# The end of a typed graph layer on one core: three stages become one stage whose engines work at different node blocks

## What is computed

```
h = relu(layernorm(x))
# per node: attention over incoming edges, softmax per edge type (6 relations, 4 heads); acc = sums over edges
t     = sum over present relations of acc / max(number present, 1)
trans = t @ Wa[type of node] + ba[type of node]            # 3 node types
out   = trans * alpha + h * (1 - alpha)                    # alpha = sigmoid(skip)[type of node]
norm  = layernorm(out) * ln_g[type] + ln_b[type]
x     = x + where(node has a message, norm, h)
h     = relu(layernorm(x))                                 # the next layer gathers rows of this h
```

## Time and profile before

| | us |
|---|---|
| median of 3 runs | 10156.97 (10148.26 to 10159.42) |
| profiled execution, its own time | 10223.11 |
| span of that execution | 10221.3 |

### The profile page before, as it was taken

One profiled execution on the slowest core, in us unless ns is written; L12 is line 12 of the kernel. 1 busy time (PEld: TensorE's weight loads), 2 busy tenths in 40 slices (PEclk: granted clock), 3 DMA queues, 4 the chain that ended last, 5 costly groups with the idle time before them and its releaser, 6 DMA issues. The chain is left out here.

```text
span 10221.3 us, 116388 instructions
## 1 busy us (share of the span) xinstructions
PE 6248.8 (61%) x25078; PEld 4724.2 (46%) x25079; DVE 5154.4 (50%) x8812; ACT 2241.4 (22%) x5049; POOL 4139.8 (41%) x4373
## 2 busy tenths in 40 slices
PE   4966676665434544788888888445555544555554
PEld 2545555554233333455555555344444433444443
DVE  3147777774323323555555555534444454444445
ACT  1211222211300000233333333322222222222221
POOL 0034554440076666333333333054444424444442
PEclk9977777777666666899999999766666666666666
DMA  2246666653032233333333333133333323333332
GB/s 91 97 148 180 189 192 175 188 170 84 12 98 86 86 92 86 99 102 102 102 104 107 102 102 103 41 111 100 99 96 100 101 54 100 101 98 103 102 102 72
DMA packets 439678, 1093.31 MB, mean 107 GB/s; under 512 B 102452, under 2 KB 177296, under 8 KB 439410
## 3 DMA queue, kind: packets, MB, share of 16 engines
q0 software_dynamic: 249344, 763.23, 26.9%
q1 hardware_dynamic: 190180, 328.60, 9.7%
HBM read 1009.55 MB, written 81.94 MB: 107 GB/s over the span
## 5 line engine op out<-in xcount | busy, mean ns | idle before, releaser
L781 POOL DMA_INDIRECT st_rows<-g_table,st_stage_idx x1632 | 1560.0, 956 | 1691.5 <-DVE st_msg L2339 1217.0
L2504 PE MATMUL st_psM<-st_msg,st_hot 128*128 128x273 f32 x3264 | 966.8, 458 | 423.1 <-DVE st_msg L2339 347.6
L882 POOL DMA_INDIRECT st_rows<-kv_table,st_stage_idx x832 | 827.5, 995 | 893.1 <-PE st_psM L1226 614.5
L2490 PE MATMUL st_psE<-st_side_alpha,st_hotrow 128*128 128x16 f32 x3264 | 694.9, 360 | 622.1 <-issue 605.1
L1831 PE MATMUL st_psC<-st_w,st_rT 128*128 128x256 f32 x3264 | 900.0, 423 | 225.5 <-ACT st_rT L1792 193.7
L2490 PEld LDWEIGHTS st_psE<-st_side_alpha,st_hotrow 128*128 128x128 f32 x3264 | 718.9, 328 | 674.4 <-issue 656.9
L2504 PEld LDWEIGHTS st_psM<-st_msg,st_hot 128*128 128x128 f32 x3264 | 714.7, 225 | 632.8 <-issue 238.2
L781 POOL DMA_INDIRECT st_rows<-h_table,st_stage_idx x816 | 832.5, 1020 | 429.1 <-issue 238.3
L712 POOL DMA_INDIRECT st_rows<-p_table,st_stage_idx x816 | 847.6, 1039 | 303.0 <-issue 221.2
L1831 PEld LDWEIGHTS st_psC<-st_w,st_rT 128*128 128x128 f32 x3264 | 634.3, 204 | 624.1 <-ACT st_rT L1792 403.0
L1727 DVE TENSOR_TENSOR st_pre<-st_psP,st_rows 128x512 f32<-128x512 f32 x816 | 526.9, 685 | 646.8 <-PE st_psP L1825 439.3
(11 more groups left out here) (407 smaller groups left out, 10111.2 us busy)
## 6 DMA issues: line engine op xcount, KB each, us to landing
st_dst_row<-in_dst_row SPq DMA_DIRECT2D x310, 512.0 KB
kv_table<-st_rows_out SPq DMA_DIRECT2D x25, 1560.0 KB, 5.6
st_ea<-in_ea SPq DMA_DIRECT2D x103, 256.0 KB
st_rows<-g_table,st_stage_idx POOLq DMA_INDIRECT x1632
st_pens<-pen_table SPq DMA_DIRECT2D x208, 72.0 KB
st_rows<-kv_table,st_stage_idx POOLq DMA_INDIRECT x832
st_rows<-h_table,st_stage_idx POOLq DMA_INDIRECT x816
st_rows<-p_table,st_stage_idx POOLq DMA_INDIRECT x816
```

Source lines behind the costliest of these rows:

```text
L781: pool.indirect_dma_start(out=rows[:, slot, j, :], out_offset=None, in_=table, in_offset=bass.IndirectOffsetOnAxis(ap=stage_idx[:, g, u * ...
L882: pool.indirect_dma_start(out=rows[:, slot, j, :], out_offset=None, in_=kv_table, in_offset=bass.IndirectOffsetOnAxis(ap=stage_idx[:, g, u ...
L2490: last = nc.tensor.matmul(expanded[:, j, u, :], onehots[:, j, :], alphas.rearrange("p n h -> p (n h)"), start=(fresh and j == 0), stop=Tru ...
L2504: last = nc.tensor.matmul(out[:, 0:MSG_W], onehots[:, j, :], msg[:, n, j, :], start=(j == 0), stop=(j == SLOTS - 1))
```

## The change

`typed_combine`, `finish_typed`, the `norm_stats` behind it and `store_normed` become one stage. Its loads go out in another order: the open values first, then half of the ends, `NODE`, `X` and the four arrays on SP's queue; the other half of the ends and all weights on ACT's queue. Each kind has its own semaphore. The sum over six relations becomes three additions. The scatter into `NODE` stays. Behind it every engine runs through 34 turns, unrolled; in turn k it works at block k minus a lag that differs by operation (PE 0, 1, 4; ACT 0, 1, 3, 4, 7, 8; DVE 2, 3, 5, 6, 7; POOL 3, 5), with two buffers each of `tm`, `tT`, `psT`, `psY` and `psG`. The choice between norm and `h` is made by multiplying with `has_msg` or `no_msg`; POOL does three elementwise operations a block. The product by `Wa` takes factors that already hold `alpha`, and the bias rows are scaled by it once. Type rows are used in place instead of copied. The store of the new `h` is the last step of a block. In the excerpt the indentation is shortened.

```diff
-  def typed_combine():
...
-    sp.dma_start(NODE[:, :, 0:SUM_W], acc_table[0:NPAD, :].rearrange("(b p) d -> p b d", p=P)).then_inc(S["node_in"], 16)
...
-    sp.dma_start(values[:, :, :, :].rearrange("s n r d -> s (n r d)"),
-          open_table.rearrange("s n d -> s (n d)")).then_inc(S["values"], 16)
-    sp.dma_start(X[:, :, :], a["x"].rearrange("(b p) d -> p b d", p=P)).then_inc(S["values"], 16)
-    sp.dma_start(src_idx[:, 0:NT], a["src"]).then_inc(S["values"], 16)
-    sp.dma_start(weight[:, 0:NT], a["weight"]).then_inc(S["values"], 16)
-    sp.dma_start(dst_rel[:, :], dst_rel_table).then_inc(S["values"], 16)
-    sp.dma_start(first[:, :], first_table).then_inc(S["values"], 16)
-    sp.wait_ge(S["values"], 16 * 6)
...
-      v.tensor_reduce(comb[:, side, D:SUM_W], values[:, side, :, D:SUM_W].rearrange("s r d -> s d r"), AX.X, ALU.add)
-      last = v.tensor_reduce(comb[:, side, 0:D], scaled[:, :, :].rearrange("s r d -> s d r"), AX.X, ALU.add)
...
-    with dve.Fori(0, NB) as b:
-      link.turn()
-      dve.wait_ge(S["h"], START + b + 1)
-      link(v.tensor_scalar(mix[:, :], h[:, block_of(b), :].squeeze(1), beta[:, ds(b, 1)], None, ALU.mult))
-      dve.wait_ge(S["trans"], START + b + 1)
-      v.scalar_tensor_tensor(NODE[:, block_of(b), 0:D].squeeze(1), psY[:, 0:D], alpha[:, ds(b, 1)], mix[:, :],
-                 ALU.mult, ALU.add).then_inc(S["mixed"], 1)
-      dve.wait_ge(S["mixed"], START + b + 1)
-    block_stats(dve, link, NODE, stat, mv)
-    v.tensor_scalar(std[:, :], mean_var[:, :, 1], LN_EPS, None, ALU.add).then_inc(S["var"], 1)
...
-    link(v.tensor_tensor(sums, sums, h[:, :, :], ALU.subtract))
-    link(v.tensor_tensor(sums, sums, has_msg[:, :].unsqueeze(2).to_broadcast([P, NB, D]), ALU.mult))
-    link(v.tensor_tensor(sums, sums, h[:, :, :], ALU.add))
-    link(v.tensor_tensor(X[:, :, :], X[:, :, :], sums, ALU.add))
...
-  def store_normed():
...
+h = st.sb("h", [P, 4, D])
+h2 = st.sb("h2", [P, 3, D])
...
+psT = [st.ps(f"psT{n}", [P, 1024]) for n in range(2)]
+psY = [st.ps(f"psY{n}", [P, 512]) for n in range(2)]
+psG = [st.ps(f"psG{n}", [P, 512]) for n in range(2)]
+ps_flag, ps_coef, psM = psT[0], psG[0], psY
...
+def turns():
+  for k in range(NB + LAST + 1):
+    yield k, lambda lag, k=k: [k - lag] if 0 <= k - lag < NB else []
...
+    sp.dma_start(values[:, :, :, :].rearrange("s n r d -> s (n r d)"),
+          open_table.rearrange("s n d -> s (n d)")).then_inc(S["values"], 16)
+    ends_in(sp, 0)
+    sp.dma_start(NODE[:, :, 0:SUM_W], acc_table[0:NPAD, :].rearrange("(b p) d -> p b d", p=P)).then_inc(S["node_in"], 16)
+    sp.dma_start(X[:, :, :], a["x"].rearrange("(b p) d -> p b d", p=P)).then_inc(S["x_in"], 16)
+    sp.dma_start(src_idx[:, 0:NT], a["src"]).then_inc(S["late"], 16)
+    sp.dma_start(weight[:, 0:NT], a["weight"]).then_inc(S["late"], 16)
+    sp.dma_start(dst_rel[:, :], dst_rel_table).then_inc(S["late"], 16)
+    sp.dma_start(first[:, :], first_table).then_inc(S["late"], 16)
+    for b in range(NB):
+      sp.wait_ge(S["h2"], START + b + 1)
+      sp.dma_start(h_table[b * P:(b + 1) * P, :], h2[:, b % 3, :]).then_inc(S[f"h_out{b % 3}"], 16)
+    sp.wait_ge(S["late"], 16 * 4)
+    for n in range(3):
+      sp.wait_ge(S[f"h_out{n}"], 16 * len(range(n, NB, 3)))
...
+    pool.wait_ge(S["prep"], START + 1)
+    for k, block_at in turns():
+      for b in block_at(3):
+        pool.wait_ge(S["h"], START + b + 1)
+        nc.gpsimd.tensor_tensor(kept[:, :], h[:, b % 4, :], no_msg[:, b:b + 1].to_broadcast([P, D]),
+                    ALU.mult).then_inc(S["kept"], 1)
+        pool.wait_ge(S["kept"], START + b + 1)
+        nc.gpsimd.tensor_tensor(rows_of(X, b), rows_of(X, b), kept[:, :], ALU.add).then_inc(S["xh"], 1)
+        pool.wait_ge(S["xh"], START + b + 1)
+      for b in block_at(5):
+        pool.wait_ge(S["part"], START + b + 1)
+        pool.wait_ge(S["affine_used"], START + b + 1)
+        nc.gpsimd.tensor_tensor(rows_of(X, b), rows_of(X, b), rows_of(NODE, b), ALU.add).then_inc(S["x_added"], 1)
...
+    ends_in(act, 1)
+    act.dma_start(skip[:, :], a["skip"].partition_broadcast(P)).then_inc(S["w_in"], 16)
+    act.dma_start(skip_col[:, :], a["skip"].unsqueeze(1)).then_inc(S["w_in"], 16)
...
+    act.wait_ge(S["w_in"], 16 * 9)
+    nc.scalar.activation(skip_col[:, :], skip_col[:, :], ACT.Sigmoid).then_inc(S["sk"], 1)
     nc.scalar.activation(skip[:, :], skip[:, :], ACT.Sigmoid).then_inc(S["sk"], 1)
+    act.wait_ge(S["sk"], START + 2)
+    nc.scalar.activation(ba[:, :], ba[:, :], ACT.Copy, scale=skip_col[:, 0:1]).then_inc(S["bias"], 1)
     act.wait_ge(S["prep"], START + 1)
-    with act.Fori(0, NB) as b:
-      for t in range(TYPES):
-        last = nc.scalar.activation(tm[:, t, :], NODE[:, block_of(b), 0:D].squeeze(1), ACT.Copy,
-                      scale=rn3[:, t, ds(b, 1)])
-      last.then_inc(S["tm"], 1)
-      act.wait_ge(S["trans"], START + b)
-      nc.scalar.copy(hot3[:, :], type_rows[:, ds(b * P, P)]).then_inc(S["hot"], 1)
-      act.wait_ge(S["tT_ps"], START + b + 1)
-      nc.scalar.copy(tT[:, :, :].rearrange("p a c -> p (a c)"), psT[:, 0:6 * P]).then_inc(S["tT"], 1)
-      normed(act, h[:, block_of(b), :].squeeze(1), b).then_inc(S["h"], 1)
-    act.wait_ge(S["var"], START + 1)
-    nc.scalar.activation(std[:, :], std[:, :], ACT.Sqrt).then_inc(S["std"], 1)
-    act.wait_ge(S["norm_ready"], START + 1)
-    with act.Fori(0, NB) as b:
-      act.wait_ge(S["affine"], START + b)
-      nc.scalar.copy(hot3[:, :], type_rows[:, ds(b * P, P)]).then_inc(S["hot"], 1)
-      nc.scalar.activation(NODE[:, block_of(b), 0:D].squeeze(1), NODE[:, block_of(b), 0:D].squeeze(1),
-                ACT.Identity, bias=shift[:, ds(b, 1)], scale=rs[:, ds(b, 1)]).then_inc(S["normed"], 1)
+    act.wait_ge(S["x_in"], 16)
+    for k, block_at in turns():
+      for b in block_at(0):
+        if b >= 2:
+          act.wait_ge(S["tT_ps"], START + b - 1)
+        for t in range(TYPES):
+          last = nc.scalar.activation(tm[:, b % 2, t, :], rows_of(NODE, b), ACT.Copy, scale=share[:, t, b:b + 1])
+        last.then_inc(S["tm"], 1)
+      for b in block_at(1):
+        act.wait_ge(S["tT_ps"], START + b + 1)
+        if b >= 2:
+          act.wait_ge(S["trans"], START + b - 1)
+        nc.scalar.copy(tT[:, b % 2, :, :].rearrange("p a c -> p (a c)"), psT[b % 2][:, 0:6 * P]).then_inc(S["tT"], 1)
+        if b >= 4:
+          act.wait_ge(S["mixed"], START + b - 3)
+          act.wait_ge(S["xh"], START + b - 3)
+        nc.scalar.activation(h[:, b % 4, :], rows_of(X, b), ACT.Relu, bias=nmr[:, b:b + 1],
+                  scale=rstd[:, b:b + 1]).then_inc(S["h"], 1)
+      for b in block_at(3):
+        act.wait_ge(S["var1"], START + b + 1)
+        nc.scalar.activation(std1[:, b:b + 1], std1[:, b:b + 1], ACT.Sqrt).then_inc(S["std1"], 1)
+      for b in block_at(4):
+        act.wait_ge(S["norm_ready"], START + b + 1)
+        nc.scalar.activation(rows_of(NODE, b), rows_of(NODE, b), ACT.Identity, bias=shift[:, b:b + 1],
+                  scale=rs[:, b:b + 1]).then_inc(S["normed"], 1)
+      for b in block_at(7):
+        act.wait_ge(S["var2"], START + b + 1)
+        nc.scalar.activation(std2[:, b:b + 1], std2[:, b:b + 1], ACT.Sqrt).then_inc(S["std2"], 1)
+      for b in block_at(8):
+        act.wait_ge(S["nmr2"], START + b + 1)
+        if b >= 3:
+          act.wait_ge(S[f"h_out{b % 3}"], 16 * (b // 3))
+        nc.scalar.activation(h2[:, b % 3, :], rows_of(X, b), ACT.Relu, bias=nmr[:, b:b + 1],
+                  scale=rstd[:, b:b + 1]).then_inc(S["h2"], 1)
...
+      half = RELS // 2
+      link(v.tensor_tensor(part[:, 0:half, :], part[:, 0:half, :], part[:, half:RELS, :], ALU.add))
+      link(v.tensor_tensor(part[:, 0, :], part[:, 0, :], part[:, 1, :], ALU.add))
+      last = v.tensor_tensor(comb[:, side, 0:D], part[:, 0, :], part[:, 2, :], ALU.add)
...
+    v.tensor_tensor(share[:, :, :], share[:, :, :], nrel[:, :].unsqueeze(1).to_broadcast([P, TYPES, NB]),
+            ALU.mult).then_inc(S["prep"], 1)
+    for k, block_at in turns():
+      for b in block_at(2):
+        dve.wait_ge(S["h"], START + b + 1)
+        dve.wait_ge(S["trans"], START + b + 1)
+        v.scalar_tensor_tensor(rows_of(NODE, b), h[:, b % 4, :], beta[:, b:b + 1], psY[b % 2][:, 0:D],
+                   ALU.mult, ALU.add).then_inc(S["mixed"], 1)
+      for b in block_at(5):
+        dve.wait_ge(S["normed"], START + b + 1)
+        dve.wait_ge(S["affine"], START + b + 1)
+        v.scalar_tensor_tensor(rows_of(NODE, b), rows_of(NODE, b), has_msg[:, b:b + 1], psG[b % 2][:, 0:D],
+                   ALU.mult, ALU.mult).then_inc(S["part"], 1)
+        dve.wait_ge(S["xh"], START + b + 1)
+        v.scalar_tensor_tensor(rows_of(X, b), psG[b % 2][:, D:2 * D], has_msg[:, b:b + 1], rows_of(X, b),
+                   ALU.mult, ALU.add).then_inc(S["affine_used"], 1)
+      for b in block_at(2):
+        dve.wait_ge(S["mixed"], START + b + 1)
+        v.bn_stats(stat1[:, :], rows_of(NODE, b)).then_inc(S["bn1"], 1)
```

(56 more changed lines are left out.)

331 lines of the change are left out of this document (136 added, 195 removed).

## The result

In one launch, back to back: the changed kernel 10009.98 us (9974.67 to 10028.13, 4 runs), the kernel before 10155.85; ratio 0.9853 [0.9825, 0.9881]. That is -146 us where -197 were forecast. So the whole profiles are 248 us apart, and only stretches of them are compared here.

A forecast was written before the change was run, and what follows sets the result against it. Blocks passed from hand to hand in series bound the old stage; PE, at 4.6 us a turn, would bound the new one. Terms -172.9 - 9.7 - 2.3 - 17.5 + 5.1 = -197.3 took 10156.97 to 9960 us, range 9932 to 9996.

The forecast's parts named there:

- Turns in place of loops: From `prep` to the weighted pass: overlapped turns of 4.6 us set by PE, 134.5 us against 307.4, -172.9.
- The drain: End of the new stage: the last block's remaining steps after its product on PE, 12.5 us.
- DVE and POOL block each other: Rival, 13%: in the turns DVE and POOL wait for each other, DVE's turn 5.6 to 6.1 us, +25, total 9985.
- Loads: Opening of the typed stage: reordered loads let the first scaling start 43.5 us after the stage's start, not 61.0; -17.5.
- The bounds 26 and 53: Earliest and latest scaling start under the load term: all ends early, 26 to 27 (-34.5); halves delayed further, 53 (-8).
- Gap: Between scatter and first turn: barrier, opening, weight loads and factors, 11.6 us, shrink to 1.9; -9.7.
- sum over relations: Ahead of the scatter: three additions replace the reduction, -3.8, and seven operations for `alpha` add 1.5; together -2.3 us.
- opening: Start of the kernel: POOL clears 48 and raises 38 semaphores, 6.3 to 6.8 us in place of 1.5; +5.1.
- Unrolled code is costed at nothing: Assumption for the new stage's 34 unrolled turns: no cost for instruction fetches, as the unrolled scatter shows no gap.

The follow-up runs named there:

- pad128: Changed kernel with bias, gain and type rows zero-padded from 3 to 128 partitions; 8164.54 us, ratio 0.9776 to the kernel before.
- ends_first_split: Changed kernel with SP's half of the ends loaded ahead of the open values, these cut into 96 and 6 rows; 8143.95 us, ratio 0.9752 to the kernel before.
- before_moved: Kernel before with 258 one-element memsets ahead of VectorE's wait for the ends; 8351.96 us, ratio 1.0003 to the kernel before.
- after_moved: Changed kernel with 254 one-element memsets ahead of VectorE's wait for the ends; 8178.1 us, ratio 0.9796 to the kernel before.

## Why the prediction missed

*Turns in place of loops*, -172.9 forecast: right in mechanism and nearly in size. PE is the bound at the high clock and waits for no other engine. The turn was mis-sized, 4.88 for 4.6, 21 times 0.28 = 5.9; all from `prep` on is 4.8 over. The sum took the pair of three-row bias products at 0.43, as one more pair of 128 rows; it is those that pause (pad128: 4.54). The kernel before had the answer, 0.62 for the same pair, one line from those in the earlier trace rows. (The drain is said to go through seven lags and lists six numbers; they and the rest make the 12.5.)

*DVE and POOL block each other*: hardly. The shift on DVE, which reads two operands, takes 0.32 beside a POOL operation and 0.16 where none overlaps it; small operations with one operand take 0.14 to 0.15 beside the same POOL operation, and DVE is busy 58 of 100 us. Nothing was held for the 0.6 of a POOL operation, and as PE never waits, it costs nothing.

*Loads*, scaling at 43.5: measured 46.7. The coefficients were the right gate, and the ends behind the open values on SP's queue the right cause. Wrong was that ACT's half is free, and the ends landed at 33.5, not at 29; 13.2 of computing follow, as forecast. The bounds 26 and 53 held, and ends_first_split, which cuts the load, reaches 24.4.

*Gap, sum over relations, opening*: 1.8 for 1.9, 16.4 for 16.4, +4.9 for +5.1. The scatter came out 1.2 shorter, with a clock of 0.95 against 0.92. All these together are 6.5 of the 50.

*The step that failed* is the sentence "Unrolled code is costed at nothing: the scatter is unrolled too and shows no gap". With it the sum carried over every pass outside the stage as it was. The sentence holds within the stage, and it asked only about the stage. By my count the new stage adds VectorE some 258 instructions ahead of the GAT layers, and a loop there now fetches part of itself in each pass: 81 packets of instructions instead of 5, and 15 stalls of 3.4 to 4.2 us. Shown is that position turns this on and off, and that it costs 15 to 17 us in total where the kernel before takes 8350. On the chips of 10150, where the forecast was made, my estimate from the layers is 15 to 45 us, and the result's own pair stands at the low end, 15 to 31. The 45 us lost outside the stage are thus fetches in part, perhaps wholly. That the fetches are there is settled, but their share of this miss is not; the rest may be chance between executions, in which passes alike in code differed by tens of microseconds (the weighted pass 1239 to 1282).

None of the rows that I read could have told: the 127 packets of the kernel before look harmless.

## What to carry to other kernels

A change of one stage moves the code of all later ones: count the packets of the instruction queue by stage before and after, and if a loop waits on issue once a pass, shift it by some dozens of harmless instructions, placed where the engine waits anyway, before judging the edit. A stage that engines share at different blocks goes at the pace of the densest engine, here 6% slower than forecast (4.88 against 4.6), since a pause between products was not read from the rows. Small loads on which a chain depends belong ahead of a large load with an awkward number of rows, on every queue, and the large one is worth cutting so that most of its rows are a multiple of 16, as 96 and 6 here.

## What the runs showed of the hardware

- A 2.5 MB load of 102 rows issued on SP's queue holds the second small load on ACT's queue too, for 22.5 us; behind the small ones, cut into 96 and 6 rows, it lands in 19.6 us instead of 35.
- Products with weights of three rows between such of 128 make a turn 0.34 us longer than with the same operands padded by zeros to 128 rows (4.88 in the changed kernel, 4.54 in pad128).
- Instruction fetches can stall VectorE 3.4 to 4.2 us a pass in a loop, by its position, and straight code too: the 258 memsets of before_moved paused 1.1 and 1.7 us, the 254 of after_moved 5.7 and 3.6 us, 128 instructions apart. The Trainium skill (Runtime: NRT & Kernel Launch, "Instruction fetch mechanics") says that a taken branch to a target outside the pages held forces a fetch before execution goes on. The stalls fit that; no run here shows how much is held.
- The same program takes 8350 us on some chips and 10150 on others. The gathers differ (kv 1498 and 1735, weighted pass 1085 and 1268, GAT layers 2368 and 3460), the stage without gathers does not (454.4 and 455.1).
